# The routers of the third and last layer move into the tail of the causal attentions

## The reference

```
xn = _layernorm(x)
s = attention(xn)
g = _silu(ffn(xn))
x = x + s * g
```

```
scores = sigmoid(x @ w_gate.T)                  # 16 scores a token
group_scores = top_k(scores by 4 groups, 2).sum(-1)
allowed = the 2 best groups
idx = top_k(scores where allowed, 4)
w = scores[idx] / (scores[idx].sum(-1) + 1e-6)
```

## Time and profile before

| | us |
|---|---|
| three runs, median (lowest, highest) | 2099.49 (2098.7, 2104.21) |
| the profiled execution, its time | 2113.85 |
| its span, first to last instruction | 2112.0 |
| attention of layer 2, from the last `maxima` on | 46.2 |
| from its output projection to the stream | 36.7 |
| attention of layer 3, from the last `maxima` on | 52.5 |
| from its output projection to the stream | 31.7 |

### The profile page before, as it was taken

The page is one execution under the profiler, slowest core; times in us unless marked ns, Lnnn a source line. Parts: engine busy times, 40 slices in busy tenths (PEclk is TensorE's granted clock), DMA queues, the critical chain, the costliest instruction groups (busy, mean ns, idle before and its releaser), DMA issues. The chain is left out here.

```text
span 2112.0 us, 33478 instructions
## 1 busy us (share of the span) xinstructions
PE 1636.7 (77%) x12275; PEld 785.5 (37%) x12287; DVE 1256.8 (60%) x2588; ACT 899.9 (43%) x1728; POOL 476.1 (23%) x404
## 2 busy tenths in 40 slices
PE   2658984599888888884757989849957988859997
PEld 1446542234333333332323444334423434243333
DVE  3212237777668666844167888154476888048888
ACT  1012333266566565562423666612224666622221
POOL 0320242766556655630030000000010000000000
PEclk7567996599989999897877999869967999769999
DMA  6012204775666566530042110000051010000000
GB/s 187 26 62 67 70 24 151 187 188 142 164 155 167 151 160 165 145 99 11 25 126 46 31 32 17 1 1 0 7 167 45 18 32 17 1 1 0 0 0 20
DMA packets 211250, 153.62 MB, mean 73 GB/s; under 512 B 57449, under 2 KB 192025, under 8 KB 210970
## 3 DMA queue, kind: packets, MB, share of 16 engines
q1 hardware_dynamic: 202426, 135.35, 24.6%
q10 hardware_dynamic: 6624, 12.06, 1.9%
q0 software_dynamic: 2048, 4.20, 0.7%
HBM read 83.47 MB, written 67.37 MB: 71 GB/s over the span
## 5 line engine op out<-in xcount | busy, mean ns | idle before, releaser
L1814 DVE TENSOR_REDUCE a1a_partial<-a1a_room 128x4 f32<-128x1024 f32 x192 | 225.9, 1220 | 31.1 <-PE a1a_room L1879 30.5
L1773 ACT ACTIVATE a1a_probsT<-a1a_st 128x512 f32<-128x512 f32 (+1 forms) x416 | 205.3, 577 | 20.3 <-PE a1a_st L1912 19.8
L2236 ACT ACTIVATE a3a_probsT<-a3a_st 128x512 f32<-128x512 f32 (+2 forms) x320 | 155.3, 562 | 118.7 <-PE a3a_st L2298 74.1
L2236 ACT ACTIVATE a2a_probsT<-a2a_st 128x512 f32<-128x512 f32 (+2 forms) x320 | 155.4, 561 | 109.3 <-PE a2a_st L2298 67.1
L2153 DVE TENSOR_REDUCE a3a_maxima<-a3a_room 128x2 f32<-128x1024 f32 (+3 forms) x160 | 170.2, 1113 | 35.2 <-PE a3a_room L2269 23.4
L2153 DVE TENSOR_REDUCE a2a_maxima<-a2a_room 128x2 f32<-128x1024 f32 (+3 forms) x160 | 170.2, 1113 | 28.5 <-PE a2a_room L2269 19.1
L1949 PE MATMUL a1a_ctx<-a1a_probsT,a1a_vpad 128*9 128x512 f32 (+3 forms) x1408 | 149.0, 523 | 1.5
L1678 POOL TENSOR_TENSOR a1a_shifted<-a1a_shifted,a1a_best 128x1024 f32<-128x1024 f32 x64 | 121.6, 1901 | 105.1 <-DVE a1a_best L1820 105.0
L1879 PE MATMUL a1a_room<-stack 48*128 48x128 bf16 (+1 forms) x1376 | 111.0, 270 | 43.6 <-DVE a1a_partial L1814 22.8
L1810 DVE CUSTOM_DVE_ANT_0 a1a_shifted<-a1a_room,a1a_bands 128x256 f32<-128x256 f32 x256 | 93.5, 421 | 84.6 <-PE a1a_room L1879 79.3
L1776 ACT ACTIVATE a1a_probsT<-a1a_st 128x512 f32<-128x512 f32 x128 | 73.7, 602 | 129.4 <-PE a1a_st L1921 129.3
(11 more groups left out here) (495 smaller groups left out, 3327.3 us busy)
## 6 DMA issues: line engine op xcount, KB each, us to landing
a1a_bands<-a_band SPq DMA_DIRECT2D x112, 192.0 KB, 4.0
a_near<-a1a_shifted SPq DMA_DIRECT2D x112, 192.0 KB, 3.0
a1a_near<-a_near SPq DMA_DIRECT2D x64, 256.0 KB, 4.1
a_band<-a1a_r_mix SPq DMA_DIRECT2D x64, 254.0 KB, 3.6
stack<-q SPq DMA_DIRECT2D x96, 96.0 KB
stack<-k SPq DMA_DIRECT2D x32, 96.0 KB
l_inputs<-l_zeros SPq DMA_DIRECT2D x1, 2624.0 KB, 9.4
f_x<-l_inputs SPq DMA_DIRECT2D x8, 320.0 KB, 5.5
```

Source lines behind the costliest of these rows:

```text
L1773: nc.scalar.activation(dst, src, ACT.Exp).then_inc(exp_done, 1)
L1814: nc.vector.tensor_reduce(partial[:, g % 2, :, 1 + r].rearrange("p (a s) -> p a s", a=2), src, X_AXIS, ALU.max).then_inc(job_free, 1)
L2236: nc.scalar.activation(probsT[:, block_at % BLOCK_ROOMS, place:place + heads, lo:], src, ACT.Exp).then_inc(exp_done, 1)
```

## The change

The router's work becomes jobs of the attention. `GroupRouter` (layer 2) has seven: four that turn the weights, one for the logits, two that spread the gates. `SoftmaxRouter` (layer 3) has five: the logits with the biases, two that turn the gates whole, two that spread them. They stand in the planner's list behind the last `maxima`; jobs behind the logits wait in the planner for `CHAIN_NS`. The choice runs on VectorE inside the attention. ScalarE's exponential of the router stands two `st` steps behind the logits in its order. The sigmoid becomes an exponential, an addition and a reciprocal. The logits of a token are written as 64 columns (layer 2, zero columns of the weight tile) or 32 (layer 3, the weights twice), where they were 16. GpSimd fills `pick` and takes the weights of layer 3 apart; `router_w` and `router_b` are loaded with the other expert weights, first of them. The gates' parts have 48 columns instead of 128. The phases of before between projection and stream are gone.

```diff
+class TailRouter:
+    E, K, WAIT_STEPS = 16, 4, 2
...
+    def logits(self, pe, dst, weight):
+        for t in range(NT):
+            mm = self.nc.tensor.matmul(dst[:, t * self.WIDTH:(t + 1) * self.WIDTH], self.k.xnT[:, t * P:(t + 1) * P], weight, start=True, stop=True)
+        return mm
...
+    def scalar(self, act):
+        act.wait_ge(self.read, 1)
+        score = self.tile["score"]
+        self.nc.scalar.activation(score[:], score[:], ACT.Exp).then_inc(self.exp_done, 1)
+
+    def turn_parts(self, pe, dst, half):
+        pe.wait_ge(self.split, 1)
+        for t in range(NT // 2):
+            mm = self.nc.tensor.matmul(dst[0:3 * self.E, t * P:(t + 1) * P], self.parts[:, half * NT // 2 + t, :], self.k.ident_bf[:], start=True, stop=True)
+        return mm
...
+class GroupRouter(TailRouter):
+    WEIGHTS, LOGITS, SPREAD = range(0, 4), 4, range(5, 7)
+    JOBS, WIDTH = 7, 64
+    PE_NS, DVE_NS, CHAIN_NS = 4 * [1800.0] + [3800.0] + 2 * [900.0], 4 * [1300.0] + [500.0] + 2 * [1300.0], 4 * [0.0] + [37000.0] + 2 * [0.0]
...
+    def tensor(self, pe, n, dst, job_free, first):
+        if n in self.WEIGHTS:
+            if n == 0:
+                pe.wait_ge(*self.landed)
+            for at, (tile, i) in enumerate(self.own_blocks(n)):
+                mm = self.nc.tensor.transpose(dst[:, at * P:(at + 1) * P], tile[:, i * P:(i + 1) * P], self.k.ident[:])
+            return mm
+        if n == self.LOGITS:
+            pe.wait_ge(job_free, first + 1)
+            return self.logits(pe, dst, self.turned[:, 0:self.WIDTH])
+        return self.turn_parts(pe, dst, n - self.SPREAD[0])
+
+    def vector(self, dve, n, src, job_free, count):
...
+        if n == self.LOGITS:
+            score, gates, G, E = self.tile["score"], self.tile["gates"], self.G, self.E
+            nc.vector.tensor_scalar(score[:], self.first_columns(src), -1.0, 80.0, ALU.mult, ALU.min).then_inc(job_free, 1)
+            dve.wait_ge(job_free, count)
+            dve.sem_inc(self.read, 1)
+            chain = Chain(dve, self.steps)
+            dve.wait_ge(self.filled, 2)
+            dve.wait_ge(self.exp_done, 1)
+            chain(nc.vector.tensor_scalar(score[:], score[:], 1.0, None, ALU.add))
+            chain(nc.vector.reciprocal(score[:], score[:]))
...
+class SoftmaxRouter(TailRouter):
+    LOGITS, WHOLE, SPREAD = 0, range(1, 3), range(3, 5)
+    JOBS, WIDTH = 5, 32
+    PE_NS, DVE_NS, CHAIN_NS = [4200.0] + 2 * [1800.0] + 2 * [900.0], [900.0] + 4 * [1300.0], [25000.0] + 4 * [0.0]
...
+    def pool(self, pool):
+        self.nc.gpsimd.tensor_copy(self.pick[:], over(self.k.pick16[0:3 * self.E, :], 2, P)).then_inc(self.filled, 1)
+        pool.wait_ge(*self.landed)
+        for a in range(2):
+            for e in range(0, self.E, 4):
+                self.nc.gpsimd.tensor_copy(self.each[:, a, e:e + 4], self.w_up[:, e:e + 4, :, a]).then_inc(self.filled, 1)
...
+            nc.vector.tensor_copy(self.gate_bias[:], src[:, CHUNK:CHUNK + E]).then_inc(self.steps, 1)
+            nc.vector.tensor_scalar(self.up_bias[:], src[:, CHUNK + E:CHUNK + 2 * E], 1.0, None, ALU.add).then_inc(self.steps, 1)
...
+            nc.vector.tensor_tensor(gates[:], self.first_columns(src), over(self.br[:], 1, NT), ALU.add).then_inc(job_free, 1)
+            dve.wait_ge(job_free, count)
+            best, _, hot = choose(nc, self.k, chain, self.choice, gates, E, self.K)
+            chain(nc.vector.tensor_tensor(score[:], gates[:], over(best[:, :, 0], 2, E), ALU.subtract))
+            chain.mark(self.read)
+            chosen = sum_hot(nc, chain, hot, self.K)
+            dve.wait_ge(self.exp_done, 1)
...
+    wr, br = ph.sb("wr", [P, E]), ph.sb("br", [P, E])
+    return (w_up, w_down, bias, down_bias, wr, br), [
+        (wr[:], w["router_w"]), (br[:], every_partition(w["router_b"])),
         (w_up[:].rearrange("p e i a -> p e (i a)"), w["gate_up_proj"].rearrange("e h f -> h e f")),
...
         jobs.append(("maxima", UNITS - 1, 1))
+        jobs += [("router", 0, n) for n in range(router.JOBS)]
...
+            if waiting and (waiting[0][1] <= max(now, read[-ROOMS]) or not jobs or jobs[0][0] == "router" and waiting[0][1] <= chain_done):
...
+                elif job[0] == "router":
+                    job_at = max(job_at, chain_done + latency)
...
+        if event == ("router", 0, router.LOGITS):
+            owed.append((router.WAIT_STEPS, event))
...
+                    if what == "router":
+                        dve.wait_ge(job_done, J + 1)
+                        router.vector(dve, n, src, job_free, J + 1)
...
                     nc.gpsimd.tensor_copy(vpad[b][:, :, :, 0:DH], heads[:, b * TILES:(b + 1) * TILES, i * HG:(i + 1) * HG, :]).then_inc(v_ready, 1)
+                    if U == UNITS // 2 - 1:
+                        router.pool(pool)
```

More of the change, by code:

```diff
@@ L658, in _ @@
                 nc.scalar.activation(p[:], logits[:], ACT.Exp).then_inc(exp_ready, 1)
[L661 to L695, removed]
 class Stream:
@@ L2042, in work_order @@
             job, job_at = None, 1e12
-            if waiting and (waiting[0][1] <= max(now, read[-ROOMS]) or not jobs):
+            if waiting and (waiting[0][1] <= max(now, read[-ROOMS]) or not jobs or jobs[0][0] == "router" and waiting[0][1] <= chain_done):
                 job, job_at = waiting[0][0], max(waiting[0][1], read[-ROOMS] + latency)
@@ L2084, in work_order @@
                 wide = what != "max"
+                if what == "router":
+                    jobs.pop(0)
+                    now += router.PE_NS[n]
+                    read.append(max(read[-1], now + latency) + router.DVE_NS[n])
+                    if router.CHAIN_NS[n]:
+                        chain_done = read[-1] + router.CHAIN_NS[n]
+                    continue
                 if what == "max":
@@ L2104, in causal_attention @@
     order = work_order()
-    jobs = [event for event in order if event[0] in ("max", "maxima", "context")]
+    jobs = [event for event in order if event[0] in ("max", "maxima", "context", "router")]
     act_order, owed = [], []
@@ L2236, in _ @@
                         nc.scalar.activation(probsT[:, block_at % BLOCK_ROOMS, place:place + heads, lo:], src, ACT.Exp).then_inc(exp_done, 1)
+                    if what == "router":
+                        router.scalar(act)
                     if what == "copy":
@@ L2248, in _ @@
                     q_stack, k_stack = stack[U % len(stack)]
-                    if what in ("max", "maxima", "context"):
+                    if what in ("max", "maxima", "context", "router"):
                         dst = room[J % ROOMS]
@@ L2275, in _ @@
                                          start=True, stop=True).then_inc(job_done, 1)
+                    if what == "router":
+                        router.tensor(pe, n, dst, job_free, jobs.index(("router", 0, 0))).then_inc(job_done, 1)
                     if what == "context":
@@ L2736, in rotary_attention @@
             prologue(nc, k, "a2j", loads, plan, stack, stacked, stored, last_parts)
[L2737 to L2738 removed]
+        with phase(nc, "r2") as pr:
+            router = make_router(pr)
+            causal_attention(nc, k, "a2a", queries, keys, values, vpad.tiles, stack, stacked, stored, after, router)
+            project_out(nc, k, "a2o", woT[:])
+            experts(router)
 class Tables:
```

294 lines of the change are left out of this document (131 added, 163 removed).

## The result

The changed kernel takes 2080.62 us (median of 4 runs, 2078.54 to 2090.31), the kernel before in the same comparison 2101.85: a ratio of 0.9892, 95% interval 0.9864 to 0.9921. Some 21 us were gained where 45 were forecast; the time lies above the range. The profiled execution took 2078.54 us, 2076.7 of span.

The account below looks back on a forecast made before the run. VectorE was taken to bound the first pass, and a relay without overlap the gaps before the streams. -71.2 + 10.2 + 12.7 + 2.5 + 0.8 = -45.0 us from the 2099.5 median gave 2054, range 2040 to 2071.

Parts of the forecast that it names:

- What is removed: Gaps between output projection and expert stream, third and last layer: 35.9 and 30.8 us go, 71.2 with warmer stream starts.
- the warm start: Start of both expert streams: 2.4 GHz instead of 1.2 behind a busy projection, 1.9 + 2.6 = 4.5 us saved.
- The third layer's block: Third attention's tail: weight turns and logits back to back on TensorE, 9.6 us; 10.2 us added with spreads, less 0.5.
- the 0.5 that the loop was to absorb: Third layer's tail: waits in the TensorE and ScalarE loop take up 0.5 us of the added router work.
- The last layer: Last attention's tail: logits 4.6, ScalarE's wait 4.5, later jobs 4.1, less 0.5, so 12.7 us added.
- the wait: Last layer's tail: ScalarE's router exponential waits for VectorE's subtraction, later exponentials queue behind it; 4.5 us, bounds 0 and 6.5.
- The clock: Last layer's tail: a low clock after TensorE's stall of about 5 us adds 2.5 us, bounds 0 and 7.
- rival 2: Router blocks bring the low clock and it stays through both tails: +18.5 us, 2073 us; chance 0.15.
- What costs nothing: VectorE's chain is covered by the tails, GpSimd's copies are free; the SP queue's delay adds 0.8 us.
- rival 1: Tails: the holes are filled, no stall or cold stretch, and no low clock over the last half unit; 2040 us; chance 0.17.
- rival 3: The spreads wait for the chain or fall behind the attention's end: up to 5 us, 2059; chance 0.03.
- rival 4: Slower than before: streams inherit the low clock, each step at least 2.5 us longer; chance 0.02.

Follow-up runs that it names:

- rows128: The changed kernel with the gate product of both expert streams put back to 128 rows, 80 of them zeros; 2063.7 us, 0.9822 of before.
- all_five: late_copies with the third layer's block spread out, the last layer's logits in 64 columns, and 27 us planned for the third layer's chain, not 37; 2048.05 us, 0.975.
- group_only: rows128 with the last layer's router, copies and stream as in the kernel before, so only the third layer's router is moved; 2084.27 us, 0.9925.
- wait8: rows128 with the last layer's router exponential eight scores' exponentials behind the logits on ScalarE, not two; 2057.95 us, 0.9782.
- before48: The kernel before with only the gate product of both streams reading 48 rows of its operands; 2127.71 us against 2104.97, ratio 1.0122.
- late_copies: wait8 with GpSimd's eight copies of the last layer's up weights made in the last unit's second pass; 2067.57 us, 0.9802.
- rows64: The changed kernel with the gate product reading 64 rows, 48 of values and 16 of zeros; 2084.79 us, 0.9913.
- w64: rows128 with the last layer's logits in 64 columns instead of 32 and a separate job for the biases; 2066.52 us, 0.9822.
- rows96: The changed kernel with the gate products reading 96 rows, 48 of values and 48 of zeros; one execution, 2075.81 us.
- spaced: wait8 with the third layer's four weight jobs and logits set apart, attention products between them; 2063.88 us, 0.9801.

## Why the prediction failed, step by step

- **What is removed** was right: both gaps closed to 0.8 us (predicted 0.9), and both streams start at the high clock.
- **The step that failed** is one that the sum does not have: it puts nothing for the gate product's operands, which the change cuts from 128 rows to 48, though the kernel runs 96 of these products in the streams. The account of the change names the 48 columns; the sum gives the streams 4.5 us for the warm start and nothing else. Against rows128, the same kernel with full operands, the narrow product costs 8.0 + 10.4 = 18.4 us of the streams; alone in the old kernel it costs 15.3 in the profile and 22.7 between medians. That is nearly the whole of the region's miss (45.0 - 25.9 = 19.1); the other parts are each within about 2 us of the forecast and nearly cancel. A row of before could have warned: a load of `f_g` takes 99 ns and sits under an `f_b` pass of 0.6 us, so its price was nothing only as long as it stayed there. The Trainium skill (TensorE: Matmul & The Clock Gate, Why this matters for your kernels) says that a single product of 32 contraction rows takes the same time as one of 128. The trace agrees for the product itself (387 and 379 ns), and not for the stream around it. The Trainium skill (TensorE: Matmul & The Clock Gate, The mechanism, in Part 3) says that a weight load is pulled ahead of running products when its row group does not conflict with theirs or when it goes to the background weight buffer. Which of these a load of 48 or 64 rows between full ones misses it doesn't say; that it starts late, the runs show.
- **The third layer's block** was costed at 9.6 us and took 8.5; the two spreads 1.07. The tail grew by 13.8 us instead of 10.2. In all_five, where the block is spread out and all of its work and the spreads too are in the tail, it grew by 11.3 at nearly the same clock (0.76, 0.77). So about 2.5 us are the lost overlap: ScalarE had nothing for 7.66 us, and the 0.5 that the loop was to absorb were no discount. The 1.7 that are left over block and spreads stand beside a lower clock than before's (0.85) and are not shown by a run of their own.
- **The last layer**: logits 5.21 us (predicted 4.6; 3.85 to 4.38 in six other profiles), the wait 3.25 (4.5), the tail 12.5 longer than before's (12.7 + 2.5). That it came near is partly luck, since before's tail was itself long by the low clock: against group_only's 45.6 us it grew by 19.1. wait8 gives the wait as 3.6 us of the tail.
- **The clock** was the right worry, but the sum has a term for it in the last layer alone. In the third layer the tail had 0.85 and 0.89 without the router (before, before48) and 0.64 to 0.78 in all twelve profiles with it; in the last layer 0.67, 0.70 and 0.89 without (before48, before, group_only), 0.68 to 0.84 with it. And it varies between executions: with the same third-layer program the tail took 60.1 or 60.2 us at 0.77 in wait8, group_only, late_copies and rows64, and 66.7 or 66.8 at 0.64, which is the lower level for 72% of it, in rows128, w64 and rows96. That is rival 2 in some executions, not in the kernel after's profile. What decides between the two was not found; rows128 and wait8 have the same instructions up to there.
- **What costs nothing**: the chain ended 22.5 us after its start and was covered, as predicted. SP's first rows of maxima went out 19.7 us behind the last attention's first reduction, 18.6 before: 1.1 for the 0.8. GpSimd's copies were not free: some 1.7 us of first pass by the means above. The prediction had this as "at most some 2 us" and left it out of the sum.
- **Rivals**: rival 1 is out, the stall is there; rival 3 did not happen in the kernel after (it did in spaced, at 4 us for the predicted 5); rival 4 is out. None held the stream's loss, and so the range had no room for it: its upper end was set by clocks and waits. With the operands at 128 rows the kernel takes 2063.7 us (rows128), inside the range.

Shown by runs: the price of the narrow product (there and back, and by rows), the wait, the lost overlap, the cover of the spreads; less sharply, from few executions, the copies. Only argued: that the late loads are what stretches the three intervals of a step (they appear and go together). Open: why 64 rows are dear and 96 are not, and why the clock falls at the changes of chunk with the narrow product.

## What to carry to other kernels

When a change narrows an operand to save zeros, look at what its neighbours in the TensorE queue are, and count the places where it runs: a product of 48 or 64 rows between full ones took hardly longer itself here (387 and 379 ns), but its weight load and the next one came out from under the products before them. When work moves into another stage's idle engine, list all its instructions, also those on the busy engine, and keep them apart from each other: one block of them (8.5 us here) left the second engine idle for most of its length (7.66). Compare profiles from a common event on, and look at the granted clock of a stretch before its length is put down to an edit.

## What the runs showed of the hardware

- The clock at the last stream's changes of chunk, after TensorE's 2 us of waiting, fell at 8 of 9 with the narrow product and at 1 of 33 with one of 96 or 128 rows.
- Weight loads with 48 or 64 rows between products of 128 rows waited 0.75 us each for "issue", with 96 or 128 rows 0.24 us; the products' own times are 387 and 379 ns, and a step of the third layer's stream 3.09 and 2.79 us. The full load behind the narrow one was late too: it began with its product, where it began 0.21 us ahead behind a full one.
- The same program's tail took 60.1 or 60.2 us at a granted clock of 0.77 in four executions and 66.7 or 66.8 at 0.64 in three, with nothing between.
- A block of 32 products took 3.79 us with 64 columns in both layers, at a granted clock of 1.00 (14 of 14); 3.85 to 5.21 with 32 and 5.10 and 4.19 with 16, where the clock fell inside the block each time (9 of 9).
- VectorE instructions of 0.17 us took up to 0.58 beside GpSimd copies of 0.64, and up to 0.98 beside one of 1.89.
